# Two-layer graph network on one core: the MLP's products in the edge stage as pairs of 128x64 column tiles

## The reference

```python
h = jnp.maximum(_layernorm(x, axis=-1), 0.0)
# layer 0: an MLP on (mean of the incoming edges' features, h)
agg = segment_sum(edge_features, tgt, 6250)
agg = agg / jnp.maximum(counts, 1.0)[:, None]
hid = relu(concatenate([agg, h], axis=1) @ W1 + b1)      # 64+256 -> 512
x = x + hid @ W2 + b2                                    # 512 -> 256
h = jnp.maximum(_layernorm(x, axis=-1), 0.0)
# layer 1: mean of the neighbours' rows
summed = segment_sum(h[src], dst, 6250)
x = x + h @ w_self.T + b_self + (summed / maximum(deg, 1)[:, None]) @ w_neigh.T
```

## Time and profile before

| | |
|---|---|
| three timed runs | 1147.02, 1150.40, 1151.46 us, median 1150.4 |
| span of the profiled execution (its own time) | 1162.0 us |
| PE busy | 1093.1 us, 94%, 11380 matmul records |
| PE weight loads | 792.0 us, 68% |
| DVE busy | 788.8 us, 68% |
| ACT busy | 491.8 us, 42% |
| POOL busy | 531.4 us, 46% |
| mean granted TensorE clock | 0.982 |
| largest groups of PE in the edge stage | L1037 140.4 us, L994 104.2 us, L982 91.8 us |

### The profile page before, as it was taken

How to read it: one execution, slowest core, us unless ns; L and a number is a source line. 1 busy time by engine, 2 the same in 40 slices (tenths; PEclk the granted TensorE clock), 3 DMA queues, 4 the chain that set the end, 5 groups by cost and what they waited for, 6 DMA issues and landing times.

```text
span 1162.0 us, 29643 instructions
## 1 busy us (share of the span) xinstructions
PE 1093.1 (94%) x11380; PEld 792.0 (68%) x11380; DVE 788.8 (68%) x1849; ACT 491.8 (42%) x957; POOL 531.4 (46%) x502
## 2 busy tenths in 40 slices
PE   3789999999999997899989999999999999999998
PEld 2667777777777775566666666676666666666665
DVE  6777878887864768665656666666666666666662
ACT  5445636333114464444343444444444444444441
POOL 3010111110003662676566666766667666667620
PEclk9799999999999999899999999999999999999999
DMA  8766655555561220233223233333333333333310
GB/s 259 215 210 202 191 159 163 163 156 162 174 220 46 73 74 27 73 98 90 87 81 89 87 96 94 89 92 91 91 96 92 88 99 89 93 90 96 95 35 19
DMA packets 72618, 131.93 MB, mean 114 GB/s; under 512 B 12414, under 2 KB 32594, under 8 KB 72492
## 3 DMA queue, kind: packets, MB, share of 16 engines
q1 hardware_dynamic: 51820, 75.25, 20.9%
q0 software_dynamic: 20672, 55.00, 16.6%
HBM read 117.25 MB, written 12.95 MB: 112 GB/s over the span
## 4 chain that ended last, share of the span: by engine, by line
PE 85%; DVE 7%; issue 2%; DVEq 2%; ACT 2%; DMA 2%; another core or an unknown queue 1%; ACTq 0%; SPq 0%
PE bank L1214 33%; PE couples L1207 10%; PE couples L1037 9%; PE bank L1233 7%; PE bank L982 7%; PE bank L994 6%; PE bank L1245 3%; PE bank L976 2%; PE bank L1225 2%; PE couples L1042 2%; DVE oreg L1645 1%; PE couples L947 1%; DMA kreg<-in_edge_attr_dram 1%; PE couples L982 1%; DVE oreg L1394 1%
## 5 line engine op out<-in xcount | busy, mean ns | idle before, releaser
L1214 PE MATMUL bank<-hreg,areg 128*128 128x512 f16 x1862 | 458.8, 384 | 0.0
L627 POOL DMA_INDIRECT wide<-h_table,aggn x332 | 363.9, 1096 | 202.7 <-PE couples L1207 122.0
L845 ACT ACTIVATE areg<-couples 128x784 bf16<-128x784 f32 x304 | 249.3, 823 | 380.3 <-PE couples L1207 336.5
L1214 PEld LDWEIGHTS bank<-hreg,areg 128*128 128x128 bf16 x1862 | 240.4, 144 | 96.0 <-issue 2.6
L1645 DVE TENSOR_TENSOR hids<-iota,kreg 128x1024 bf16<-128x1024 f16 (+1 forms) x304 | 177.5, 625 | 134.2 <-PE couples L1207 123.3
L1645 DVE TENSOR_TENSOR oreg<-iota,kreg 128x1024 bf16<-128x1024 f16 (+1 forms) x304 | 177.4, 625 | 39.2 <-PE couples L1207 29.5
L1037 PEld LDWEIGHTS couples<-oreg,kreg 128*64 128x64 f32 x3232 | 119.0, 144 | 65.2 <-issue 64.1
L1037 PE MATMUL couples<-oreg,kreg 128*64 128x48 f32 x3232 | 140.4, 232 | 21.5 <-DVE oreg L1394 17.5
L595 POOL TENSOR_TENSOR xr<-xr,b2bc 128x512 f32 x25 | 33.6, 1342 | 223.4 <-ACT h0buf L717 223.4
L1394 DVE TENSOR_TENSOR oreg<-iota,wide 128x384 f32<-128x384 f32 x202 | 122.9, 609 | 4.4 <-issue 1.3
L994 PE MATMUL bank<-wide,hids 128*128 128x256 f32 x400 | 104.2, 398 | 0.0
(11 more groups left out here) (176 smaller groups left out, 1117.4 us busy)
## 6 DMA issues: line engine op xcount, KB each, us to landing
kreg<-in_edge_attr_dram SPq DMA_DIRECT2D x202, 256.0 KB, 2.8
h_table<-hreg SPq DMA_DIRECT2D x25, 256.0 KB
xr<-in_x_dram SPq DMA_DIRECT2D x6, 1024.0 KB, 6.9
wide<-h_table,aggn POOLq DMA_INDIRECT x332
out_dram<-hbuf SPq DMA_DIRECT2D x38, 128.0 KB
out_dram<-h0buf SPq DMA_DIRECT2D x10, 128.0 KB
wide<-in_L_gnn_W_dram SPq DMA_DIRECT2D x2, 512.0 KB, 8.9
hids<-h_table,aggn POOLq DMA_INDIRECT x64
```

The costliest lines, as they stand in the source:

```text
L627: pool.indirect_dma_start(near_rows(n % RING, w), None, table, bass.IndirectOffsetOnAxis(ap=nearsrc[:, k:k + 1], axis=0)).then_inc(s_rows[ ...
L845: act.activation(step.rearrange("p (a k) -> p a k", a=2), cpl[s % 2][:, :, 0:BC * KEYS], ACT.Copy).then_inc(s_adj, 1)
L1214: ins = pe.matmul(bank[4 + par], adj[:, par, :, h], htab[:, h, :], start=(h == 0), stop=(h == TN - 1))
```

## The change

Beside the edge groups, `hidden` and `outer` get `beside=True`. Each 128x128 product is split into two products of 64 weight columns, which write partitions 0 to 63 and 64 to 127 of the same bank. The mean edges' part is no longer two 64-row tiles ahead of q = 0: each call takes all 128 rows of `w1a` (which holds W1's 64 rows twice) against all 128 partitions of `aggn[:, q, :]`, of which the half that isn't written stays zero from a memset on POOL at the start. Spans 2 to 5 are written out on PE. Units without groups beside them keep the old form.

```diff
+            pool.memset(aggn[:, :, :], 0.0)
             pool.memset(acc[:, :], 0.0).then_inc(s_const, 1)
...
+            def halves_of(beside):
+
+                return (slice(0, FE), slice(FE, P)) if beside else (slice(0, P),)
...
-                    for e in qs:
-                        pe.matmul(hidden_bank(e, k, own)[:, b * NM:(b + 1) * NM], w1a[e * FE:(e + 1) * FE, cols],
-                                  aggn[e * FE:(e + 1) * FE, e, :], start=True, stop=False)
+                    if not beside:
+                        for e in qs:
+                            pe.matmul(hidden_bank(e, k, own)[:, b * NM:(b + 1) * NM], w1a[e * FE:(e + 1) * FE, at:at + P],
+                                      aggn[e * FE:(e + 1) * FE, e, :], start=True, stop=False)
...
+                into = hidden_bank(q, k, own)[:, b * NM:(b + 1) * NM]
+                if beside:
+
+                    for m in halves_of(beside):
+                        pe.matmul(into[m, :], w1a[:, at + m.start:at + m.stop], aggn[:, q, :], start=True, stop=False)
                 for h in range(DH):
-                    ins = pe.matmul(hidden_bank(q, k, own)[:, b * NM:(b + 1) * NM], w1b[:, h, cols],
-                                    h0T[:, bass.ds(2 * u, 2), h, :], start=False, stop=(h == DH - 1))
+                    for m in halves_of(beside):
+                        ins = pe.matmul(into[m, :], w1b[:, h, at + m.start:at + m.stop],
+                                        h0T[:, bass.ds(2 * u, 2), h, :], start=False, stop=(h == DH - 1))
...
-                    ins = pe.matmul(bank[6 + q][:, t * D:(t + 1) * D], hids[:, q, b, t * P:(t + 1) * P], w2s[:, b, :],
-                                    start=(b == 0), stop=(b == HB - 1))
+                    for m in halves_of(beside):
+                        ins = pe.matmul(bank[6 + q][m, t * D:(t + 1) * D], hids[:, q, b, t * P + m.start:t * P + m.stop],
+                                        w2s[:, b, :], start=(b == 0), stop=(b == HB - 1))
...
-                            part(i, *which)
+                            part(i, *which, beside=True)
...
-                loop(pe, lambda k: span(k, k - 1), 2, XPARTS)
+                for k in range(2, XPARTS):
+                    span(k, k - 1)
```

More of the change, by code:

```diff
@@ L958, in edge_sums, with hidden @@
                 return ins
-            def hidden(i, k, b, q, own=0):
-                cols = slice((2 * k + b) * P, (2 * k + b + 1) * P)
+            def halves_of(beside):
+                return (slice(0, FE), slice(FE, P)) if beside else (slice(0, P),)
+            def hidden(i, k, b, q, own=0, beside=False):
+                at = (2 * k + b) * P
                 if q == 0:
@@ L980, in hidden, with outer @@
                 u = 2 * i + q
+                into = hidden_bank(q, k, own)[:, b * NM:(b + 1) * NM]
+                if beside:
+                    for m in halves_of(beside):
+                        pe.matmul(into[m, :], w1a[:, at + m.start:at + m.stop], aggn[:, q, :], start=True, stop=False)
                 for h in range(DH):
-                    ins = pe.matmul(hidden_bank(q, k, own)[:, b * NM:(b + 1) * NM], w1b[:, h, cols],
-                                    h0T[:, bass.ds(2 * u, 2), h, :], start=False, stop=(h == DH - 1))
+                    for m in halves_of(beside):
+                        ins = pe.matmul(into[m, :], w1b[:, h, at + m.start:at + m.stop],
+                                        h0T[:, bass.ds(2 * u, 2), h, :], start=False, stop=(h == DH - 1))
                 if b == 1:
                     ins.then_inc(s_hidp[q], 1)
-            def outer(i, q, t, half):
+            def outer(i, q, t, half, beside=False):
                 if t == 0:
```

## The result

The changed kernel takes 1140.7 us (median of 5; 1139.3 to 1146.3) against 1150.4; the ratio is 0.9936, interval 0.9918 to 0.9955. It is faster, by some 7 us (by the ratio) to 10 us (by the medians) where 19 were forecast. Run again beside the kernel before on another chip, the ratio was 0.9868 (0.9837 to 0.9899), 13.6 us between the medians; the two intervals don't meet, so the size of the gain on the whole kernel isn't fixed by these runs.

The account below looks back on a forecast made before the run. PE (TensorE) was taken to pace the edge stage, with DVE next. PE's 27.6 us less, 8.2 given back by DVE and 0.5 by edge loads made 19 us less: 1150.4 to 1131 us, range 1120 to 1143.

Parts of the forecast that it names:

- (a): MLP pieces on PE: paired column tiles run side by side, 0.864 instead of 1.15 us each; 32.0 and 2.2 us less.
- rival D: Pieces and mean edges on PE: the two column tiles don't overlap; 1244 us; chance 0.06.
- Rival C: Column-tile pairs on PE: each waits 0.05 us for its weight loads, kernel time stays the same; chance 0.04.
- (b): Mean edges on PE: 128 weight rows, half against zeros, cost 0.864 instead of 0.63 us a block; 6.6 us more.
- (c): Four spans written out on PE: 0, bounds -1 and +2 us; the added POOL memset of 0.52 us stays hidden.
- (d): DVE late where its load is thickest in each stretch: 8.2 us given back; bounds 0 and twice that.
- (e): Edge loads in a ring of six, late only behind loads of x: 0 to 2 us more, taken as 0.5.
- The stages behind move forward as a block: Stages behind 344 us start from flags of the edge stage, so they move forward with it, their lengths unchanged.
- Rival B: DVE or the loads behind x take most of PE's gain: 16 and 2 us back, 1141 us; chance 0.13.

Follow-up runs that it names:

- e11: Changed kernel with the mean edges as two 64-row tiles again, the rest in column tiles; one run of 1159.1 us.
- e1: Kernel before with PE's spans 2 to 5 written out, nothing else changed; ratio 0.999.
- e2: Changed kernel with only the second product (outer) in column tiles, hidden and mean edges as before; ratio 0.9945.
- e6: Changed kernel with DVE's heavy parts (inverses, statistics) moved by one step, all work kept; ratio 0.9888.
- e4: Changed kernel with POOL's addition of b2 cut to 8 of 256 columns; ratio 0.9835.
- e7: e6, with POOL's addition of b2 also waiting for the one-hot just ahead of an inverse; ratio 0.9825.
- e5: Kernel before with POOL's addition of b2 cut to 8 of 256 columns; ratio 0.9932.
- e8: e7, with each load of x from part 2 on issued in three pieces between the edge loads; ratio 0.9804.
- e3: Changed kernel with all products of the left column tile ahead of the right one's in each piece; one run of 1169.0 us.
- e9: e8, with the last two pieces of the edge stage as 128x128 products again; ratio 0.9721.
- e10: Changed kernel run again, its file unchanged, beside e9 on the same chip; 1151.2 us against 1164.8 for the kernel before.

## Why the prediction was wrong

The direction, the mechanism and PE's account (a to c) were right; the size was not. The edge stage became 12.4 us shorter where 19 were forecast, and the kernel 7 to 10 us in the first comparison, about half of the forecast or less. The second comparison had 13.6 us. That 1140.7 lies in the stated range, 2 us from its upper end, rests on the wide range more than on the working.

- (a) Two column tiles with 256 f32 columns on one bank run side by side: right, 0.86 to 0.90 us a piece (0.864 forecast). Pairs stand 0.216 us apart. This refutes rival D. Rival C (chance 0.04) had each pair wait 0.05 us for its weight loads, half of the first record's 0.48 less 0.38 us, my estimate. No run shows such a wait: in the piece at 209.42 us of the changed kernel the eight weight loads stand between 209.39 and 210.03 us, 0.14 us each, beside the records of the products (to 210.48), and the pairs are still 0.216 us apart.
- (b) The mean edges cost 2 x 0.46 = 0.92 us a block instead of 0.864. I took their form as given; e11 shows a stage 3 to 4 us shorter with the old form.
- (c) Writing out: 0, as forecast, by e1. The memset stayed hidden, it took 0.52 us and ended at 5.85 us.
- **(d) is the step that failed**: "what is late next: DVE", sized at 8.2 us by one place and 0 elsewhere. The stops behind DVE grew by 13.2 us. At the place that was sized (j = 14 and 16) it was 9.6 us less the 3.1 there before, 6.5 and so less than forecast. But j = 9 (3.5 us more) and j = 21 and 22 (3.2 more) stop PE too, 6.7 us that had no term; only the upper bound ("twice that, because the other parts also come to within a few per cent of balance") took them in. I compared sums over five groups, and assumed that where the sums leave room there is no stop.
- What the runs showed in its place: the unit that matters is a single step (e2, e6). A part of 0.75 to 1 us between one-hot j and one-hot j + 1 makes that one-hot late. The stop was 0.4 to 0.8 us where one of the two groups ahead has no piece beside it (j = 9, 16 and 21), and about 0.3 where both have one (j = 17 and 20 in e6; e6's stop at 18 stands behind the shorter means product). At j = 14 both have one, and PE stops for 0.67 us because POOL holds the one-hot: the stop goes in e4 and e7 and stays in e6. The 1.52 us one-hot stood in the trace of before, inside the 8.92 us from which (d) was worked out; I read all of them as DVE's own work and didn't ask what lengthened it. e4 and e5 give what POOL's addition costs: 1.68 us a typical stretch after the change, 0.58 before.
- (e) 0.5 us for the edge loads: the stops at j = 0, 3, 6 and 18, where they and the steps behind them show, grew by about 2.3 us. The faster PE got, the more they cost (4.5 us of waits in e4), until e8 took them away.
- "The stages behind move forward as a block": nearly, as far as the order shows. POOL's first load of places came 11.2 us earlier (351.0 against 362.2); the stage began 0.4 us later, and some 0.8 us were lost at PE's branch. Whether what follows kept its length can't be told: the profiles have 787.5 us there against 799.8 before, but the changed kernel's second profile has 796.3.

Rival B (1141 us, chance 0.13) comes closest. It gave 18 us back, the stage shows 15.5, the forecast had 8.7. That its 1141 is also the median of the first comparison is partly luck, since the stage lost 12.4 us and not B's 9.6. The argument against it, that DVE's own need of 236.7 us is below PE's 243, had two errors. PE's 243 still held 5 us of stops, and its own work after the change was 237.0, level with DVE's need. And DVE's 236.7 held POOL's part, 1.4 us in a typical stretch (0.98 + 1.52 less twice 0.55): with it gone, DVE waits 21.6 us for PE in e8's 246.3, and PE still stops for 9 us at single steps.

## What to carry to other kernels

When the engine that sets the pace gets faster, walk the next engine step by step at the depth of the buffers between them, and mark each place where its work for one step exceeds what the first engine will then have in hand; sums over a stretch hide these. Before that, look for instructions of one group whose longest is three times the median and find what ran beside them: a hold that costs little now may cost more after the change. Here it then paid to move the other engine's parts by one step, and a third engine's work to a moment that holds nobody (7.6 us of the stage from the changed kernel to e7).

## What the runs showed of the hardware that I had not expected

- Records of two column tiles overlap even when program order has all four of one tile first (e3: piece 0.89 us either way).
- A one-hot on VectorE (two f32 operands in SBUF) lasts up to 1.66 us instead of 0.55 beside GpSimd's 128x512 f32 addition. It isn't the only operation that is held: a means product took 0.69 us instead of 0.42 beside it (e6, line 1423), and one maximum of the counts 1.25 instead of 0.22 (changed kernel, line 1415). The reciprocals beside it kept their 0.94 us, the statistics their 0.43 and the window additions their 0.2, and with the addition placed beside an inverse no one-hot was over 0.56 (e7).
- A branch over some code on TensorE's sequencer took 3.7 to 5.7 us, and PE's next record came 0.28 us after its end in four profiles (changed kernel, e8, e9, e10). What it hides behind is short: the queued products of 3.2 us, at a mean granted clock of 0.59 (1.00 up to 332.7 us, 0.50 from 333.2 us to their end), left 1.9 us of idle in the changed kernel; in its repetition (e10) they took 1.9 us at 1.00 and the idle time was 3.6.
